# GNN layer pair: nodes laid across partitions by n % 128, bias by one-row products

## The chip, the core and the metric

The kernel runs on one core of a Trainium2 chip. The metric is the device time of one execution in microseconds, median of the runs. TensorE is called PE, VectorE DVE, ScalarE ACT, GpSimd POOL; SP is the engine that issues most DMAs.

## The reference

6250 nodes with 128 features, 200,000 edges sorted by destination, two residual layers in float32:

```
h = relu(layernorm(x))
ef  = (relu(edge_attr @ We1 + be1) @ We2 + be2) * sigmoid(ew * Wt + bt)
msg = relu(concat(h[src], ef) @ Wn1 + bn1) @ Wn2 + bn2
x = x + segment_sum(msg, dst) + h                     # layer 0
h = relu(layernorm(x))
agg = segment_sum(h[src], dst)
x = x + relu(relu((h + agg) @ W1 + b1) @ W2 + b2)     # layer 1
```

The kernel sums the messages before the product with Wn2, which is linear: `segment_sum(msg) = segment_sum(relu(...)) @ Wn2 + count * bn2`, where count is the number of edges that end in a node. This count times bias is one of the two things the change is about.

## The kernel before

The node features sit in SBUF as `xs` [128 partitions, NT = 49 tiles, 128 features], worked on in NG = 7 groups of GT = 7 tiles. Node n lies in partition n // 49, tile n % 49: partition p holds 49 nodes that follow one another. The sums over edges lie the other way round, features in partitions and nodes along the free axis: `acc` [128, 2, ...], where `acc[:, 0, n]` is the sum of node n and `acc[0, 1, n]` its edge count. One tile of nodes is therefore a view of `acc` with a step of 49 elements (`acc_group`).

The program has these stages; within an engine everything stands in a fixed order, and engines wait for one another on semaphores.

1. **Prologue.** SP loads `x` in 7 transfers of 448 KB (L370), then weights and index tables, all on one DMA queue. DVE takes statistics (L998), and later the window parameters (L1006 and on, which need edge bounds that went to DRAM and back); ACT normalizes (L590), PE multiplies by the node half of Wn1, DVE adds (L1034, L1038, L1042), and SP stores the product as `table0` in 7 transfers (L431). POOL gathers rows of `table0` by `src` (L525) once all are stored; SP reads tile bounds back (L434) after that too, and DVE waits for these.
2. **Layer 0 loop**, 49 bodies of four edge pairs: products, messages, one-hot sums into `acc`. For layer 1 it also counts edges per (source, destination window) in matrices `counts_d`, with keys made by `edge_keys` from the source's partition and tile.
3. **Transition.** After the last sum, ACT copies each group of `acc` into a contiguous stage (L670), PE multiplies a tile (stationary operand) by `wn2` (L857), DVE adds the product to `xs` (L1273). The counts of all nodes go by one DMA from one partition into 128 (L448, `count_n`), and DVE adds count times bias with 49 instructions (`add_bias`, L1264). DVE takes statistics (L1278). SP then reloads `acc[:, 1]` with stored count matrices (L354, 2940 KB), and POOL moves the edge keys (L562); both had waited for the DMA of the counts.
4. **Second table.** ACT normalizes again (L679), three bf16 parts of each value are made by ACT (L686), POOL (L565) and DVE (L1289, L1294), PE transposes (L866), DVE copies the transposed tile into `acc` as the new start (L1292). SP stores the parts as `table1` in 7 transfers of 672 KB through two buffers (L463); ACT may write a buffer again when its store has landed.
5. **Layer 1 loop.** PE sums gathered rows (L881) and products with count matrices (L891) while POOL gathers from `table1`.
6. **Output.** PE multiplies `w1` (stationary) with four and three tiles of `acc` as the moving operand (L937, L938), ACT applies relu (L719), PE multiplies by `w2` (L946), DVE adds (L1390, L1392), SP stores `out` (L494) in 7 transfers.

Of the kernel before, what the change touches and what calls it, by code (L numbers as in the profile page):

```python
# [10 lines left out]
ALU = mybir.AluOpType  # L11
# [3 lines left out]
P = 128  # L15
D = 128
# [70 lines left out]
def gnn_program(nc, x, ea, ew, src, src_tiles, dst_tiles, dst_blocks, We1, be1, We2, be2, Wt, bt, Wn1, bn1, Wn2, bn2,  # L87
                W1, b1, W2, b2, out):
    ctx = ExitStack()
    with ctx:  # L90
        def sb(name, shape, dt=F32):
            return ctx.enter_context(nc.sbuf_tensor(name, shape, dt))
# [25 lines left out]
        rstd = sb("rstd", [P, NT])  # L118
        count_n = sb("count_n", [P, NT])
        shift = sb("shift", [P, NT])  # L120
# [170 lines left out]

        acc_staged = sem("acc_staged")
        counts_moved = sem("counts_moved")
        x1_chain = sem("x1_chain")
        acc_zeroed = sem("acc_zeroed")
# [64 lines left out]
        def acc_group(g, which=0):  # L360

            v = acc[:, which, 0:N_PAD].rearrange("f (p t) -> f t p", t=NT)
            return v[:, bass.ds(g * GT, GT), :]


        @block.sync
        def _(sp):
            sp.dma_start(dst_b, dst_blocks).then_inc(dst_loaded, 16)
            for g in range(NG):
                sp.dma_start(xs[:, g * GT:(g + 1) * GT, :],  # L370
                             x[:, g * GT * D:(g + 1) * GT * D].rearrange("p (t d) -> p t d", d=D))\
                  .then_inc(x_loaded[g], 16)
                if g == 0:
                    sp.dma_start(dst_t[:, :], dst_tiles).then_inc(dst_tiles_loaded, 16)
# [52 lines left out]

            t0 = table0.rearrange("(p t) d -> p t d", t=NT)
            with sp.Fori(0, NG) as g:
# [17 lines left out]

            sp.dma_start(count_n[:, :], acc[0:1, 1, 0:N_PAD].rearrange("a (p t) -> a p t", t=NT)).then_inc(counts_moved, 16)  # L448

            sp.wait_ge(counts_moved, 16)  # L450
            for i in (0, 1):
# [7 lines left out]

            t1 = table1.rearrange("(p t) d -> p t d", t=NT)  # L460
            for g in range(NG):
# [28 lines left out]

            ov = out.rearrange("p (t d) -> p t d", d=D)
            with sp.Fori(0, NG) as g:
                sp.wait_ge(out_made, g + 1)
                sp.dma_start(ov[:, bass.ds(g * GT, GT), :], xs[:, bass.ds(g * GT, GT), :]).then_inc(out_stored, 16)  # L494
            sp.wait_ge(out_stored, 16 * NG)
# [3 lines left out]
        def _(pool):  # L499
# [58 lines left out]
            with pool.If(sweeps > 1):  # L558
                with pool.Fori(NBODY, sweeps * NBODY) as b:
                    gather_body(b)  # L560
            pool.wait_ge(counts_moved, 16)
            pool.tensor_copy(keys1, keys0).then_inc(keys_moved, 1)  # L562
# [14 lines left out]
        def _(act):  # L577
# [83 lines left out]
            with act.If(sweeps > 1):  # L661
                with act.Fori(1, sweeps) as s:
                    sweep(s, False)


            act.wait_ge(acc_added, sweeps * NB)
            for g in range(NG):
                if g >= 2:
                    act.wait_ge(upd_mm, g - 1)
                act.activation(stages[g % 2], acc_group(g), ACT.Copy).then_inc(acc_staged, 1)  # L670

# [51 lines left out]
        def _(pe):  # L723
# [126 lines left out]


            for g in range(NG):
                pe.wait_ge(acc_staged, g + 1)
                if g >= 2:
                    pe.wait_ge(x1_made, g - 1)
                for u in range(GT):
                    i = pe.matmul(p_prod[g % 2][:, u, :], stages[g % 2][:, u, :], wn2[:, :], start=True, stop=True)  # L857
                i.then_inc(upd_mm, 1)
# [92 lines left out]
        def _(dve):  # L951
# [206 lines left out]
            def edge_keys():  # L1158

                dve.wait_ge(src_loaded, 16)  # L1160
                src_b, key = src_b0[:, 0:NTILE], key0[:, 0:NTILE]
                chain(dve.tensor_scalar(src_b, src_i, 1.0 / NT, 0.5 / NT - 0.5, ALU.mult, ALU.add))
                settle()
                chain(dve.tensor_scalar(src_b, src_b, ROUND, None, ALU.add))
                settle()
                chain(dve.tensor_scalar(src_b, src_b, ROUND, None, ALU.subtract))
                settle()
                chain(dve.scalar_tensor_tensor(out=src_t, in0=src_b, scalar=-float(NT), in1=src_i,
                                               op0=ALU.mult, op1=ALU.add))
# [89 lines left out]

            dve.wait_ge(counts_moved, 16)  # L1260

            def add_bias(g):
                for t in range(g * GT, (g + 1) * GT):
                    i = dve.scalar_tensor_tensor(out=xs[:, t, :], in0=bn2_r[:, :], scalar=count_n[:, t:t + 1],  # L1264
                                                 in1=xs[:, t, :], op0=ALU.mult, op1=ALU.add)
                i.then_inc(x1_chain, 1)

            add_bias(0)
            for g in range(NG):
                x_g = xs[:, g * GT:(g + 1) * GT, :]  # L1270
                dve.wait_ge(upd_mm, g + 1)
                dve.wait_ge(x1_chain, g + 1)
                dve.tensor_tensor(x_g, x_g, p_prod[g % 2], ALU.add).then_inc(x1_made, 1)  # L1273
                if g < NG - 1:
                    add_bias(g + 1)
                dve.wait_ge(x1_made, g + 1)
                for t in range(g * GT, (g + 1) * GT):
                    i = dve.bn_stats(stats[:, t, :], xs[:, t, :])  # L1278
                i.then_inc(x1_stats, 1)
# [150 lines left out]
```

## Time and profile before

| | us |
|---|---|
| median of 3 runs (lowest, highest) | 3589.09 (3583.87, 3596.16) |
| profiled execution: time, span | 3590.76, 3589.0 |
| mean granted TensorE clock | 0.799 |
| busy: PE 2681.7 (75%), POOL 2068.4 (58%), DVE 1962.9 (55%), ACT 1004.6 (28%) | |
| transition, last sum to last statistics | 2593.9 to 2629.1 |
| second table, to the first product of layer 1 | to 2665.7 |
| output, first product to the end of the span | 3549.5 to 3589.0 |

The span runs from the first to the last instruction. Positions are microseconds from its start. The granted clock is the share of TensorE's full 2.4 GHz: 1.00 is 2.4 GHz and 0.50 is 1.2 GHz. A float32 product of 128 columns is two MATMUL records, each with its own weight load.

### The profile page before, as it was taken

How to read it: one execution, taken by the hardware profiler on the slowest of the kernel's cores; microseconds unless marked ns; L12 is line 12 of the kernel's file. 1: busy time of each engine (PE TensorE's matmuls, PEld its weight loads, DVE VectorE, ACT ScalarE, POOL GpSimd, SP SyncE). 2: the span in 40 equal slices, each digit the busy share in tenths (PEclk: the TensorE clock that was granted, in tenths of full speed). 3: DMA queues.
4: the chain of work that ended last, by engine and by line, in shares of the span. 5: the costliest groups of instructions: out<-in, count | busy, mean ns of one | idle time of the engine just before them, and what ended most of it. 6: DMA issues, size and time to landing. Idle time of an engine off the chain costs nothing.

```text
span 3589.0 us, 51735 instructions
## 1 busy us (share of the span) xinstructions
PE 2681.7 (75%) x14584; PEld 1614.4 (45%) x14585; DVE 1962.9 (55%) x4112; ACT 1004.6 (28%) x1000; POOL 2068.4 (58%) x2104
## 2 busy tenths in 40 slices
PE   4688878788777877788777877877745767666777
PEld 2444444444444444444434443433432544544554
DVE  7655655566565666566656666665763333233333
ACT  3233333333333333333333332322231111011111
POOL 4666666666566656666666566655324556555552
PEclk8788888788887887888888888888865766767778
DMA  5444444444343444344343443433222434334332
GB/s 188 110 124 134 130 132 126 128 127 135 121 127 122 126 122 123 121 126 123 122 124 124 122 123 121 124 106 118 48 94 84 152 99 129 104 111 126 117 103 62
DMA packets 229412, 426.77 MB, mean 119 GB/s; under 512 B 82703, under 2 KB 141584, under 8 KB 229072
## 3 DMA queue, kind: packets, MB, share of 16 engines
q0 software_dynamic: 74752, 153.23, 16.3%
q1 hardware_dynamic: 103152, 177.42, 15.0%
q10 hardware_dynamic: 51266, 93.34, 7.4%
q8 instruction: 97, 1.59, 0.2%
q14 instruction: 145, 1.19, 0.1%
HBM read 364.35 MB, written 59.43 MB: 118 GB/s over the span
## 4 chain that ended last, share of the span: by engine, by line
PE 41%; issue 20%; DVE 17%; another core or an unknown queue 11%; DVEq 9%; DMA 1%; SPq 0%; ACT 0%; ACTq 0%
PE ps L891 9%; PE ps L803 9%; PE ps L762 8%; PE ps L771 5%; DVE nodes L1152 5%; PE ps L782 4%; PE ps L754 3%; DVEq L1086 2%; DVEq L1132 2%; DVE arena L1152 2%; DVE hot L1107 1%; PE ps L881 1%; DVE acc L1094 1%; DVEq L1149 1%
## 5 line engine op out<-in xcount | busy, mean ns | idle before, releaser
L525 POOL DMA_INDIRECT big<-table,idx x2080 | 2044.2, 983 | 1391.8 <-issue 588.2
L803 PE MATMUL ps<-nodes 128*128 128x500 bf16 x1280 | 461.1, 476 | 348.7 <-issue 200.0
L762 PE MATMUL ps<-arena,we 128*128 128x512 f32 x784 | 516.4, 791 | 18.5 <-issue 13.3
L611 ACT ACTIVATE big<-big 128x1024 f32<-128x1024 f32 x196 | 207.1, 1057 | 1072.0 <-DVE big L1101 932.0
L782 PE MATMUL ps<-hot,big 128*128 128x64 f32 x3136 | 391.3, 274 | 99.4 <-issue 67.2
L1152 DVE TENSOR_SCALAR nodes<-iota_k,win_off,nodes 128x500 bf16<-128x500 f16 x1280 | 453.0, 405 | 0.0
L782 PEld LDWEIGHTS ps<-hot,big 128*128 128x128 f32 x3136 | 378.0, 194 | 102.2 <-issue 100.1
L1149 DVE TENSOR_TENSOR nodes<-iota_b,nodes 128x384 bf16<-128x384 f16 (+1 forms) x492 | 244.8, 497 | 278.6 <-remote 156.9
L803 PEld LDWEIGHTS ps<-nodes 128*128 128x128 bf16 x1280 | 107.6, 106 | 589.1 <-issue 308.0
L1101 DVE TENSOR_TENSOR big<-ps,big 128x1024 f32<-128x1024 f32 x196 | 239.0, 1219 | 225.5 <-issue 217.6
L601 ACT ACTIVATE arena<-ps,cols 128x1024 f32<-128x1024 f32 x196 | 218.6, 1115 | 405.3 <-PE ps L754 222.3
L692 ACT ACTIVATE arena<-ps 128x490 f32<-128x490 f32 x96 | 100.0, 1042 | 766.3 <-PE ps L806 656.5
L1094 DVE TENSOR_TENSOR acc<-ps,acc 128x128 f32 x392 | 113.6, 290 | 292.6 <-remote 244.3
L803 PE MATMUL ps<-arena 128*128 128x500 bf16 x384 | 170.6, 554 | 136.5 <-DVE arena L1152 96.1
L891 PE MATMUL ps<-acc,nodes 128*128 128x120 f32 x1568 | 222.7, 299 | 63.5 <-issue 56.2
L634 ACT ACTIVATE arena<-ps 128x490 f32<-128x490 f32 x192 | 199.0, 1037 | 227.8 <-remote 214.8
L1149 DVE TENSOR_TENSOR arena<-iota_b,arena 128x256 bf16<-128x256 f16 x192 | 80.8, 421 | 329.3 <-PE ps L803 187.3
L754 PE MATMUL ps<-arena,we 64*128 64x512 f32 x784 | 231.6, 664 | 24.6 <-DMA win_row<-win_d 17.6
L762 PEld LDWEIGHTS ps<-arena,we 128*128 128x128 f32 x784 | 174.0, 246 | 165.1 <-issue 160.2
L891 PEld LDWEIGHTS ps<-acc,nodes 128*128 128x128 f32 x1568 | 209.8, 215 | 72.8 <-issue 72.3
L606 ACT ACTIVATE arena<-arena,cols 128x1024 f32<-128x1024 f32 x196 | 240.9, 1229 | 0.0
L771 PEld LDWEIGHTS ps<-wn1b,ef 128*128 128x128 f32 x1568 | 188.2, 196 | 80.8 <-issue 80.8
(139 smaller groups left out, 2512.4 us busy)
## 6 DMA issues: line engine op xcount, KB each, us to landing
arena<-in_ew SPq DMA_DIRECT2D x196, 512.0 KB
arena<-in_ea SPq DMA_DIRECT2D x196, 256.0 KB
counts_d<-arena ACTq DMA_DIRECT2D x192, 245.0 KB
acc<-counts_d ACTq DMA_DIRECT2D x15, 2940.0 KB
big<-table,idx POOLq DMA_INDIRECT x2080
table<-big SPq DMA_DIRECT2D x7, 672.0 KB, 3.0
idx<-in_src SPq DMA_DIRECT2D x260, 4.0 KB
xs<-in_x SPq DMA_DIRECT2D x7, 448.0 KB, 8.7
```

What stands on the lines that cost most here:

```text
L525: pool.indirect_dma_start(to(u, q, t), None, table, bass.IndirectOffsetOnAxis(ap=idx[:, u, at:at + 1], axis=0))\
L601: act.activation(hid[:, :, :].rearrange("p q c -> p (q c)"), p_hid2, ACT.Relu, bias=be1_c).then_inc(hid_made, 2)
L606: act.activation(v, v, ACT.Sigmoid, bias=bt_c, scale=wt_c).then_inc(tw_made, 2)
L754: pe.matmul(p_hid[q], we1[k, :], ea_s[k, u, :], start=True, stop=True).then_inc(hid_mm, 1)
L762: pe.matmul(p_ef[q], we2[:, :], hid[:, q, :], start=True, stop=True).then_inc(ef_mm, 1)
L771: i = pe.matmul(p_pre[q][:, t * D:(t + 1) * D], efs[m][:, q, t * P:(t + 1) * P], wn1b[:, :], start=True, stop=True)
L782: pe.matmul(p_agg[:, q, 0, :], msg[:, m, q, t, :], hot_f[:, m, q, t, :], start=(t == 0), stop=(t == TB - 1))
L803: m = pe.matmul(to, hots[:, t, :], keys[:, t, :], start=False, stop=True, skip_group_check=True)
L891: m = pe.matmul(to, nodes[:, a, :], sums[:, :, a, :], start=(a == 0), stop=(a == NT - 1))
L1101: dve.tensor_tensor(msg[:, u % 2, :, :, :].rearrange("p q t d -> p (q t d)"), p_pre2, rows[:, u, :, :, :].rearrange("p q t d -> p (q t d)" ...
L1149: dve.tensor_tensor(hots[:, h * half:h * half + n, :], iota_v.to_broadcast([P, n, P]), half_src.to_broadcast([P, n, P]), ALU.is_equal)
L1152: m = dve.tensor_scalar(keys[:, h * half + t, :], iota_k[:, :], win_off[:, bass.ds(win, 1)], key[:, h * n + t:NTILE + VP][:, bass.ds(at, 1 ...
```

## The change

Node n now lies in partition n % 128 of tile n // 128. A tile of nodes is then 128 neighbours in `acc`, and the view of a group is contiguous. PE reads the sums straight from `acc` as stationary operand, with no copy by ACT. Edge count times bias is added on PE too: to each tile's product, a product with one contraction row (`edges[0:1]`, the counts, times one row of `bn2_r`) accumulates into the same PSUM tile; the DMA of the counts and `add_bias` on DVE are gone. A partition's share of a transfer of `x`, `table0`, `table1` and `out` is no longer one run of 7 nodes but 7 runs of one node: 512 bytes each, 768 in `table1`. DRAM rows stay in node order, so gathers read the same addresses. SP's reload of `acc[:, 1]` waits for all products with the counts; POOL's copy of the keys waits for PE to have passed the last sum (`keys_free`). `edge_keys` has the same instructions with its two results exchanged.

```diff
         def acc_group(g, which=0):
-            v = acc[:, which, 0:N_PAD].rearrange("f (p t) -> f t p", t=NT)
+            v = acc[:, which, 0:N_PAD].rearrange("f (t p) -> f t p", p=P)
             return v[:, bass.ds(g * GT, GT), :]
@@ block.sync
+            x_tiles, out_tiles = (a.rearrange("p c -> (p c)").rearrange("(t p d) -> p t d", p=P, d=D) for a in (x, out))
                 sp.dma_start(xs[:, g * GT:(g + 1) * GT, :],
-                             x[:, g * GT * D:(g + 1) * GT * D].rearrange("p (t d) -> p t d", d=D))\
+                             x_tiles[:, g * GT:(g + 1) * GT, :])\
-            t0 = table0.rearrange("(p t) d -> p t d", t=NT)
+            t0 = table0.rearrange("(t p) d -> p t d", p=P)
-            sp.dma_start(count_n[:, :], acc[0:1, 1, 0:N_PAD].rearrange("a (p t) -> a p t", t=NT)).then_inc(counts_moved, 16)
-            sp.wait_ge(counts_moved, 16)
+            sp.wait_ge(upd_mm, NG)
             for i in (0, 1):
                 sp.wait_ge(c_stored[i], 16 + 16 * (NW0 // 2))
             load_sums(sp, 0)
-            t1 = table1.rearrange("(p t) d -> p t d", t=NT)
+            t1 = table1.rearrange("(t p) d -> p t d", p=P)
-            ov = out.rearrange("p (t d) -> p t d", d=D)
-                sp.dma_start(ov[:, bass.ds(g * GT, GT), :], xs[:, bass.ds(g * GT, GT), :]).then_inc(out_stored, 16)
+                sp.dma_start(out_tiles[:, bass.ds(g * GT, GT), :], xs[:, bass.ds(g * GT, GT), :]).then_inc(out_stored, 16)
@@ block.gpsimd
-            pool.wait_ge(counts_moved, 16)
+            pool.wait_ge(keys_free, 1)
             pool.tensor_copy(keys1, keys0).then_inc(keys_moved, 1)
@@ block.scalar
-            act.wait_ge(acc_added, sweeps * NB)
-            for g in range(NG):
-                if g >= 2:
-                    act.wait_ge(upd_mm, g - 1)
-                act.activation(stages[g % 2], acc_group(g), ACT.Copy).then_inc(acc_staged, 1)
@@ block.tensor
+            pe.wait_ge(acc_added, sweeps * NB)
+            pe.sem_inc(keys_free, 1)
             for g in range(NG):
-                pe.wait_ge(acc_staged, g + 1)
                 if g >= 2:
                     pe.wait_ge(x1_made, g - 1)
+                sums, edges = acc_group(g), acc_group(g, 1)
                 for u in range(GT):
-                    i = pe.matmul(p_prod[g % 2][:, u, :], stages[g % 2][:, u, :], wn2[:, :], start=True, stop=True)
+                    pe.matmul(p_prod[g % 2][:, u, :], sums[:, u, :], wn2[:, :], start=True, stop=False)
+                    i = pe.matmul(p_prod[g % 2][:, u, :], edges[0:1, u, :], bn2_r[0:1, :], start=False, stop=True)
                 i.then_inc(upd_mm, 1)
@@ block.vector
-            dve.wait_ge(counts_moved, 16)
-            def add_bias(g):
-                for t in range(g * GT, (g + 1) * GT):
-                    i = dve.scalar_tensor_tensor(out=xs[:, t, :], in0=bn2_r[:, :], scalar=count_n[:, t:t + 1],
-                                                 in1=xs[:, t, :], op0=ALU.mult, op1=ALU.add)
-                i.then_inc(x1_chain, 1)
-            add_bias(0)
             for g in range(NG):
                 x_g = xs[:, g * GT:(g + 1) * GT, :]
                 dve.wait_ge(upd_mm, g + 1)
-                dve.wait_ge(x1_chain, g + 1)
                 dve.tensor_tensor(x_g, x_g, p_prod[g % 2], ALU.add).then_inc(x1_made, 1)
-                if g < NG - 1:
-                    add_bias(g + 1)
                 dve.wait_ge(x1_made, g + 1)
                 for t in range(g * GT, (g + 1) * GT):
                     i = dve.bn_stats(stats[:, t, :], xs[:, t, :])
```

On DVE in the transition, before: `xs<-bn_r,count_n,xs` is `add_bias`, seven tiles at a time, `xs<-xs,ps` the addition of a group's product, `BN_STATS` the statistics.

```order
L1264 SCALAR_TENSOR_TENSOR xs<-bn_r,count_n,xs 128x128 x7
L1273 TENSOR_TENSOR xs<-xs,ps 128x896
L1264 SCALAR_TENSOR_TENSOR xs<-bn_r,count_n,xs 128x128 x7
L1278 BN_STATS stats<-xs 128x6 x7
L1273 TENSOR_TENSOR xs<-xs,ps 128x896
```

Now only the addition and the statistics of each group are left on DVE. On PE in the same place, the new order is, for each of 49 tiles, a product with `wn` and one with the bias row `bn_r`, both with `acc` as the other operand (before, these were 49 products `ps<-wn,big` in a row, from the stage):

```order
L840 REGISTER_ALU
L847 MATMUL ps<-wn,acc 128x128
L848 MATMUL ps<-bn_r,acc 128x128
L847 MATMUL ps<-wn,acc 128x128
L848 MATMUL ps<-bn_r,acc 128x128
```

The number of products doubles, from 49 to 98. On SP behind the layer 0 loop, before, the DMA of the counts stands ahead of the reload of `acc`, the index loads and the seven stores of `table1`:

```order
L448 DMA count_n<-acc 128x1x49
L354 DMA acc<-counts_d 128x12x490
L457 ISA
L457 DMA idx<-in_src 128x8
L463 DMA table<-big 128x2688 x7
```

And now, where the stores name 7 runs of 384 elements a partition instead of one of 2688:

```order
L444 REGISTER_ALU
L351 DMA acc<-counts_d 128x12x490
L453 ISA
L453 DMA idx<-in_src 128x8
L459 DMA table<-big 128x7x384 x7
```

The reload keeps its place in the queue, but the wait ahead of it is now for the last product of the transition.

## Rows read from the trace of the kernel before

**Rows 1.** Timeline of the prologue: start, length, engine, line, operation [idle before].

```profile
11.17 9.56 DVE L998 BATCH_NORM_STATS2 stats<-xs 128x6 f32<-128x128 f32 x49
27.25 0.56 DVE L1006 TENSOR_TENSOR big<-great_all,base_all 1x392 int32<-1x392 int32 x1 [3.86 <-DMA base_all<-base_d]
57.42 2.82 POOL L525 DMA_INDIRECT big<-table,idx  x1 [41.79 <-DMA table<-nodes]
```

**Rows 2.** Stretches of the prologue: last columns clock, DMA share, GB/s.

```profile
10.00:15.00 5.00, 0.00 (x0) 0.00 (x0) 4.97 (x23) 0.00 (x0) 5.00 (x1) 1.00 1.02 404
15.00:15.50 0.50, 0.00 (x0) 0.00 (x0) 0.50 (x4) 0.00 (x0) 0.50 (x1) 1.00 1.02 329
16.00:16.50 0.50, 0.00 (x0) 0.00 (x0) 0.50 (x4) 0.00 (x0) 0.00 (x0) 1.00 1.23 285
```

**Rows 3.** Timeline of the transition.

```profile
2593.89 3.47 ACT L670 ACTIVATE big<-acc 128x896 f32<-128x896 f32 x2 [4.31 <-DVE acc L1094]
2595.82 5.75 PE L857 MATMUL ps<-wn,big 128*128 128x128 f32 x28 [2.83 <-ACT big L670]
2596.75 0.40 SPq L354 DMA_DIRECT2D acc<-counts_d  x1
2596.78 2.81 POOL L562 COPY arena<-nodes 128x3148 f32<-128x3148 f32 x1 [15.20 <-DMA count_n<-acc]
2596.88 4.44 DVE L1264 SCALAR_TENSOR_TENSOR xs<-bn_r,count_n,xs 128x128 f32<-128x128 f32 x7 [3.02 <-DMA count_n<-acc]
...
2606.61 1.92 DVE L1264 SCALAR_TENSOR_TENSOR xs<-bn_r,count_n,xs 128x128 f32<-128x128 f32 x7
2608.44 1.44 DVE L1278 BATCH_NORM_STATS2 stats<-xs 128x6 f32<-128x128 f32 x7
2609.80 1.07 DVE L1273 TENSOR_TENSOR xs<-xs,ps 128x896 f32<-128x896 f32 x1
...
2627.66 1.45 DVE L1278 BATCH_NORM_STATS2 stats<-xs 128x6 f32<-128x128 f32 x7
```

**Rows 4.** Stretches of the transition, columns as in rows 2.

```profile
2595.00:2600.00 5.00, 4.18 (x19) 4.21 (x20) 3.12 (x3) 3.17 (x3) 2.81 (x1) 0.50 0.49 122
2600.00:2605.00 5.00, 3.37 (x24) 3.01 (x23) 4.90 (x17) 3.29 (x3) 0.00 (x0) 0.92 1.04 395
```

**Rows 5.** Groups over the whole span: busy us, mean ns; two weight loads, and two copies of the same size.

```profile
L803 PEld LDWEIGHTS ps<-nodes 128*128 128x128 bf16 x1280 | 107.6, 106 | 589.1 <-issue 308.0 <-DVE nodes L1152 240.2
L797 PEld LDWEIGHTS ps<-zeros 1*128 1x128 bf16 x288 | 26.9, 94 | 53.8 <-issue 29.7
L1292 DVE COPY acc<-ps 128x896 f32<-128x896 f32 x7 | 12.2, 1738 | 0.0
L1038 DVE COPY ef<-ps 128x896 f32<-128x896 f32 x4 | 4.3, 1082 | 0.0
```

**Rows 6.** The chain through two groups of the second table: start, length, what.

```profile
2639.37 3.00 DMA table<-big
...
2643.43 1.09 DVE big L1289
...
2647.12 3.00 DMA table<-big
```

**Rows 7.** The chain through one group of the output, and one product of the loop.

```profile
2559.85 1.91 PE ps L762 x4
...
3557.81 1.82 PE ps L937 x2
3559.63 1.37 PE ps L938 x2
...
3575.24 1.56 PE ps L946 x14
```

**Rows 8.** A stretch at the start of the output, columns as in rows 2.

```profile
3553.00:3554.00 1.00, 1.00 (x3) 0.40 (x2) 0.00 (x0) 0.90 (x1) 0.00 (x0) 0.93 0.00 0
```

**Rows 9.** PE between 2676.6 and 2711.6 us, by groups.

```profile
L891 PE MATMUL ps<-acc,nodes 128*128 128x120 f32 x18 | 5.4, 360 | 12.7 <-issue 12.3
```

More of the change, by code:

```diff
@@ L118, in gnn_program @@
         rstd = sb("rstd", [P, NT])
-        count_n = sb("count_n", [P, NT])
         shift = sb("shift", [P, NT])
@@ L290, in gnn_program @@
         out_chain = sem("out_chain")
-        acc_staged = sem("acc_staged")
-        counts_moved = sem("counts_moved")
-        x1_chain = sem("x1_chain")
+        keys_free = sem("keys_free")
         acc_zeroed = sem("acc_zeroed")
@@ L1161, in edge_keys @@
                 src_b, key = src_b0[:, 0:NTILE], key0[:, 0:NTILE]
-                chain(dve.tensor_scalar(src_b, src_i, 1.0 / NT, 0.5 / NT - 0.5, ALU.mult, ALU.add))
+                chain(dve.tensor_scalar(src_t, src_i, 1.0 / P, 0.5 / P - 0.5, ALU.mult, ALU.add))
                 settle()
-                chain(dve.tensor_scalar(src_b, src_b, ROUND, None, ALU.add))
+                chain(dve.tensor_scalar(src_t, src_t, ROUND, None, ALU.add))
                 settle()
-                chain(dve.tensor_scalar(src_b, src_b, ROUND, None, ALU.subtract))
+                chain(dve.tensor_scalar(src_t, src_t, ROUND, None, ALU.subtract))
                 settle()
-                chain(dve.scalar_tensor_tensor(out=src_t, in0=src_b, scalar=-float(NT), in1=src_i,
+                chain(dve.scalar_tensor_tensor(out=src_b, in0=src_t, scalar=-float(P), in1=src_i,
                                                op0=ALU.mult, op1=ALU.add))
```

## The prediction

> **What bounds the kernel now.** I read the timeline first, to find the places that the change touches, then for each the chain that ended last and the stretches with the granted clock and the DMA rate. Both edge loops are left as they are: gathers read the same DRAM rows, and `edge_keys` and the one-hot work have the same instructions and shapes. So the time can change in four places only: prologue, transition, second table and output, together some 160 us of the 3589.
>
> In the **transition** the last sum is in `acc` at 2593.9. PE starts on the first stage at 2595.8; DVE gets the counts at 2596.9, and its first seven bias additions take 4.44 us beside POOL's copy of the keys, against 1.92 for seven later on [rows 3]. From then on DVE has no gap: bias 1.92, statistics 1.44, addition 1.07, about 4.2 us a group with the overlaps of their ends. The last statistics end at 2627.66 + 1.45 = 2629.1. DVE is the bound there; PE and ACT wait for it.
>
> In the **second table** the chain goes round through two buffers: store 3.00, ACT, DVE L1289, DVE L1292, DVE L1294, next store, 7.75 us for two groups [rows 6]. The copy L1292 takes 1.74 us, while L1038 copies the same 896 columns out of PSUM in 1.08; the difference is the step of 49 elements in the destination [rows 5].
>
> In the **output** PE is on the chain without a gap: L937 1.82, L938 1.37, L946 1.56, so 4.75 us a group [rows 7]. L937's two instructions read 512 columns each with that same step, 0.91 us apiece, while L762 puts four instructions of 512 contiguous float32 columns into 1.91 us, with the last one's tail: about 0.43 apiece when the clock is full.
>
> **The change part by part.** Everything is summed against the profiled execution (3590.76 us, span 3589.0); the median of the three runs is 1.7 us lower.
>
> *A, loads of x.* Runs of 512 bytes instead of 3584. In the queue, big runs go at 404 GB/s from 10 to 15 us; at 15 us the weights begin, which are rows of 512 bytes, and the rate falls to 329, later to 285 as tiny columns mix in, with the engines fully busy [rows 2]. I take 320: 7 x 448 KB = 3.21 MB take 10.0 us instead of 8.0. DVE's statistics of x run without a gap from 11.2 to 20.7 and cover their own loads, even 2 us later. But everything queued behind x on SP's queue comes later too: weights, index tables, and the edge bounds, which go to DRAM and back, and on whose return DVE's L1006 waits at 27.25 [rows 1]. DVE does nothing else before that, so +2.0 us. Bounds: 0 and, at 285 GB/s, +3.3.
>
> *B, stores of table0.* They have the time of the pipeline to go out; only the last one is on the path (POOL's first gather waits for it [rows 1]): 459 KB at 320 instead of 404 GB/s, +0.3.
>
> *C, transition.* Gone: ACT's copies, the DMA of the counts, the 49 additions. Added: 98 MATMUL records for 49 one-row products. No row shows a float32 product with one contraction row. The nearest say that rows don't shorten it: a weight load of 1 x 128 takes 94 ns, one of 128 x 128 takes 106 [rows 5]. I take the full product's price; the lower bound is nothing, the upper is that a change between 1 and 128 rows stops the overlap of load and product, some 0.3 us a record. PE can begin at 2593.95. The clock has fallen to half there; before, it came back 5 us after PE began: 28 records took 5.75 us [rows 3, 4]. So 24 of the 196 records at 0.205 us until 2599, and 172 at the full clock's pace of the output, 1.56 / 14 = 0.111: 19.2 us, PE's end at 2618.2. A group is 3.1 us on PE and 2.5 on DVE (1.07 + 1.44), so DVE keeps up and adds its last group behind PE: 0.2 + 1.07 + 1.45 gives 2620.9 to 2621.2. Against 2629.1 that is **-7.9 us**. PE, not DVE, is then the bound. POOL's copy of the keys comes right at the start, where DVE is idle. The reload of `acc[:, 1]` on SP's queue moves from 2596.8 to 2618.3. Before, its 2940 KB were in at about 2606.7, ten microseconds after issue [rows 3, 4]; now they are in near 2628.5, and the first table store behind it on the queue is due at 2631.5, so this stays hidden with 3 us to spare. What waits behind it besides are four small index loads, due much later.
>
> *D, second table.* L1292 writes contiguously: -0.66 us, of which 0.43 reach L1294, since POOL's part of the group ends then. The store has 768-byte runs: from 512 bytes at 320 GB/s (25.6 ns a run on one of 16 engines) and 5376 at 404 (213 ns) a line gives 35 ns, 56 of them 1.9 us instead of 1.7, so the 3.00 become 3.27. First turn -0.43, three more at -0.43 + 0.27: **-0.9**. Bounds: -1.5 with no loss in the stores, +2 if a store lands 1 us later.
>
> *E, output.* L937 to 0.86, L938 to 0.65 us a group: -1.67. The group is then 3.08 us on PE; DVE's two additions (each the size of L1273's 1.07) stay under that. But PE comes to the output with half the clock, which rises at 3553.1, 3.5 us after the first product at 3549.5 [rows 8]. At half the clock contiguous columns would take 0.86 us an instruction, twice the 0.43, hardly less than the 0.91 of the strided ones. So the first group wins 0.2 and the second loses a little: 6 x 1.67 + 0.2 - 0.3 = **-9.9**. Bounds: -11.7 with the full clock at once, -8 if it takes twice as long.
>
> *F, last store of out.* On the path, as B: +0.3.
>
> Sum: 2.0 + 0.3 - 7.9 - 0.9 - 9.9 + 0.3 = -16.1. 3590.8 - 16.1 = 3574.7, and 1.7 less for the median: about 3574.
>
> The size of the runs is where the Trainium skill speaks otherwise: "DMA: Bandwidth & Descriptors", section Specifications, gives 512 bytes as the least transfer for line rate. By that A, B and F would be nothing and the time 3571. The row has 329 GB/s against 404, and I go by the row.
>
> **The rivals.**
>
> *The clock stays low in the transition.* PE now runs without a break, which speaks for the full clock; but before, with its breaks, it was granted 0.50 and then 0.92 in two stretches there [rows 4]. All 196 records at 0.21 us are 41 us: PE's end 2635, the statistics' 2638, C is +9 instead of -7.9, and the time 3591: no change. 6 in 100.
>
> *A pause of PE, the slower side.* PE has stretches in which it issues hardly anything and waits for nothing that the profile names. The longest stands right behind the place of the change: between 2676.6 and 2711.6 it gets through 18 products of L891 in 35 us, with 12.3 us idle put down to "issue" ahead of them [rows 9]. If such a pause falls into the transition's doubled run of products, where PE is now alone on the path, it costs its full length; from 27 us on the kernel is slower by over 0.3%, and one of 35 us gives 3609. Against it: POOL is gathering back to back in that stretch, and idle in the transition. 6 in 100.
>
> *That pause shrinks*, since PE's stream is 98 products longer ahead of it and comes to it otherwise. PE's chain goes through it, so up to 30 us more would be won: 3545 to 3565. 12 in 100.
>
> *The step is not what slows the output.* Then E is nothing, and D only the stores: 3584, no change by the measure below. For it: no row shows these two lines with another layout. Against: ACT's copy with the step takes 1.74 us and more (3.47 for two [rows 3]), DVE's 1.74, both well above their contiguous likes. 10 in 100.
>
> *Forecast*, 3574 with its own range 3567 to 3582: 62 in 100. What is left, 4, is short DMA runs that are much slower than the weights' (half rate: A +8, D +5), about 3588.
>
> **How the numbers follow.** A change of this kernel can be told from none by about 0.3%, 11 us, so faster means under 3578. The forecast's own spread leaves it there 9 times in 10: 56, and the shrunken pause 12 make 0.69. Same: the rest of the forecast 6, low clock 5, step 9, short runs 4: 0.24. Slower: 0.07. The range leaves out half of the shrunken pause and the slower side: 3559 to 3590.
>
> **What would show it.** L937's duration per instruction near 0.6 us instead of 1.1 and seven groups 3.1 us apart; L1292 at 1.08; PE's last bias product near 2618 on the scale of before, at a clock of 1.00 from 5 us after its start; the reload landed before the first store of `table1` is issued; L1006 two microseconds later. Wrong it would be if the one-row products cost more than full ones, if the stores of short runs land a microsecond or more later, or if PE's pauses fall otherwise.

## The result, and the profile after

The changed kernel takes 3636.07 us (median of five, 3627.78 to 3646.90) against 3589.09 us (3583.87 to 3597.29): a ratio of 1.0132, 95% interval 1.0103 to 1.0161. It is 47 us slower where 15 us faster was forecast, and outside the range. The profiled execution is the fastest of the five: 3627.78 us, span 3626.0 us, so the two profiles differ by 37.0 us only. The table divides these 37.0; each row is a difference between marks of the two timelines.

| stretch | forecast | measured |
|---|---|---|
| prologue, to L1006, now L997 (A) | +2.0 | +6.4 |
| from there to the first gather (B) | +0.3 | +0.5 |
| layer 0 loop | 0 | +3.8 |
| transition, last sum to last statistics (C) | -7.9 | **+38.4** |
| second table, to the first row sum (D) | -0.9 | -1.0 |
| layer 1 loop | 0 | -1.7 |
| output, with the last store (E, F) | -9.6 | -9.4 |

**Prologue.** Timeline of the changed kernel (start, length, engine, line, operation, idle before), where [rows 1] stand for the kernel before:

```profile
2.34 10.89 SPq L368 DMA_DIRECT2D xs<-in_x  x6
10.55 9.60 DVE L989 BATCH_NORM_STATS2 stats<-xs 128x6 f32<-128x128 f32 x49
13.27 1.45 SPq L374 DMA_DIRECT2D wn1a<-in_Wn  x1
23.05 0.42 SPq L386 DMA_DIRECT2D base_d<-least  x1
33.61 0.55 DVE L997 TENSOR_TENSOR big<-great_all,base_all 1x392 int32<-1x392 int32 x1 [10.82 <-DMA base_all<-base_d]
```

and a stretch of it (the last columns are the clock, the DMA share and GB/s):

```profile
6.00:14.00 8.00, 0.00 (x0) 0.00 (x0) 7.97 (x22) 0.00 (x0) 8.00 (x1) 1.00 1.14 319
```

The rate is the forecast's 320 GB/s. The statistics are not delayed. But SyncE needs 10.89 us to issue six loads of x, and only then come the weights and, at 23.05 us, the first store of block bounds. The same two rows in the kernel before:

```profile
2.17 4.47 SPq L370 DMA_DIRECT2D xs<-in_x  x6
16.43 0.42 SPq L388 DMA_DIRECT2D base_d<-least  x1
```

VectorE waits 10.8 us for the bounds, where it waited 3.9 [rows 1].

**Transition.** The same timeline at its start, and further on the addition that stands for L1273 of [rows 3]:

```profile
2603.91 0.72 DVE L1085 TENSOR_TENSOR acc<-ps,acc 128x128 f32 x2 [2.87 <-PE ps L773]
2604.77 0.77 PE L847 MATMUL ps<-wn,acc 128*128 128x128 f32 x2 [1.01 <-DVE acc L1085]
2605.47 0.50 PEld L848 LDWEIGHTS ps<-bn_r,acc 1*128 1x128 f32 x2 [0.23 <-issue]
2605.47 0.79 PE L848 MATMUL ps<-bn_r,acc 1*128 1x128 f32 x2
2606.19 0.50 PEld L847 LDWEIGHTS ps<-wn,acc 128*128 128x128 f32 x2 [0.23 <-issue]
2606.19 0.80 PE L847 MATMUL ps<-wn,acc 128*128 128x128 f32 x2
...
2675.74 1.09 DVE L1254 TENSOR_TENSOR xs<-xs,ps 128x896 f32<-128x896 f32 x1 [7.55 <-PE ps L848]
2675.78 0.38 SPq L351 DMA_DIRECT2D acc<-counts_d  x1
```

Each product has two records. A product starts every 0.72 us, from the first to the last, whichever its kind; PEld is idle 0.23 us ahead of each. From the start of the first product to that of the last record it is 70.5 us. VectorE waits 7.55 us for the last group. And the clock stayed at its lower level (1.2 GHz), as the stretches show, where [rows 4] has 0.92 within ten microseconds:

```profile
2600.00:2605.00 5.00, 3.98 (x18) 3.73 (x19) 1.61 (x3) 0.51 (x1) 0.21 (x1) 0.50 0.01 3
2605.00:2675.00 70.00, 70.00 (x195) 48.23 (x195) 15.23 (x48) 0.00 (x0) 2.59 (x1) 0.50 0.00 1
```

PE counts as busy for the whole 70 us: the busy share alone does not show that each product takes more than three times its time.

**Second table and output.** One store in the chain that ended last (start, length, what), for [rows 6]:

```profile
2695.70 3.25 DMA table<-big
```

and timeline rows for L1292 of [rows 5] and for the output's groups of [rows 7]:

```profile
2689.49 1.08 DVE L1271 COPY acc<-ps 128x896 f32<-128x896 f32 x1
...
3602.54 1.02 PE L928 MATMUL ps<-acc,w 128*128 128x512 f32 x2
...
3605.61 1.02 PE L928 MATMUL ps<-acc,w 128*128 128x512 f32 x2
```

The copy takes 1.08 us, the store 3.25, and an output group 3.07: these three steps went as forecast.

### The profile page after: what moved, and what is told of

It reads as the page before. It is cut to its first block, busy times and chain, and to the rows that moved or that the text cites. A ratio compares the mean times of both kernels' runs of the same rounds, so it can differ in the third digit from the quotient of the medians.

```text
span 3626.0 us, 51863 instructions
## 1 busy us (share of the span) xinstructions
PE 2731.1 (75%) x14682; PEld 1643.1 (45%) x14683; DVE 1945.5 (54%) x4063; ACT 992.3 (27%) x993; POOL 2066.5 (57%) x2104
## 4 chain that ended last, share of the span: by engine, by line
PE 40%; issue 20%; DVE 17%; another core or an unknown queue 11%; DVEq 10%; DMA 1%; SPq 1%; ACT 0%; POOL 0%; ACTq 0%
PE ps L882 9%; PE ps L791 8%; PE ps L750 7%; PE ps L759 5%; DVE nodes L1143 5%; PE ps L770 4%; DVEq L1077 3%; PE ps L742 3%; DVEq L1123 2%; DVE hot L1098 2%; DVE arena L1143 2%; DVE acc L1085 2%; DVEq L1140 1%; PE ps L872 1%
## 5 line engine op out<-in xcount | busy, mean ns | idle before, releaser
L770 PE MATMUL ps<-hot,big 128*128 128x64 f32 x3136 | 383.6, 274 | 80.1 <-issue 44.4
L759 PEld LDWEIGHTS ps<-wn1b,arena 128*128 128x128 f32 x1568 | 186.3, 194 | 90.9 <-issue 88.2
```

The costliest lines, as they stand in the source:

```text
L759: i = pe.matmul(p_pre[q][:, t * D:(t + 1) * D], efs[m][:, q, t * P:(t + 1) * P], wn1b[:, :], start=True, stop=True)
L770: pe.matmul(p_agg[:, q, 0, :], msg[:, m, q, t, :], hot_f[:, m, q, t, :], start=(t == 0), stop=(t == TB - 1))
```

## The experiments

Times are from four chips. The kernel before takes 2891 to 2896 us on three of them and 3659 us on the fourth, so only ratios to it, measured on the same chip, are given. The first four versions share a chip; so do 64 rows, the unaltered kernel, loads on ScalarE's queue and old runs; so do one part alone, the same with full rows, the strided operand and the split; and so do the last three. Lengths of a stretch are from the profiles, one execution each; a time for the 98 products goes from the first start to the last. Line numbers are those of the changed kernel, a few lines off in some variants.

Theory 1 was formed from the timeline above: a weight load with another number of rows than the product ahead of it waits for it, and costs a piece of time at each change. Its rivals: two products that add into one PSUM tile (2), the stationary operand read from `acc` unstaged (3), a price of every one-row product (5).

**Full rows.** The bias product takes all 128 rows; rows 1 to 127 of the counts are zero.

```diff
-  i = pe.matmul(p_prod..., edges[0:1, u, :], bn2_r[0:1, :], start=False, stop=True)
+  i = pe.matmul(p_prod..., edges[:, u, :], bn2_r[:, :], start=False, stop=True)
```

> One edit to the changed kernel: the bias product takes all 128 rows of the edge counts and of the bias (rows 1 to 127 of the counts are zero, so the sum is the same) where it took one row. Theory 1 (a change between 128 rows and one row stops the overlap of a weight load with the product before it, at every product, and the clock stays at 1.2 GHz with it): the 98 products of the transition fall from 0.72 us each (70.9 us in all) to 2 records of about 0.11 us at 2.4 GHz or 0.215 at 1.2 GHz, so 21 to 42 us, and the kernel from 3636 to 3586 to 3607 us. Theory 2 (it is that two products add into one tile of PSUM) and theory 3 (it is that the stationary operand is taken from the accumulator unstaged): no difference, 3636 us.

Measured: 2879.72 us, ratio 0.9964 (0.9949 to 0.9978). Two stretches of its transition:

```profile
2120.00:2125.00 5.00, 4.08 (x22) 4.11 (x23) 0.29 (x1) 0.00 (x0) 2.80 (x1) 0.56 0.03 7
2125.00:2145.00 20.00, 19.68 (x177) 19.49 (x175) 15.52 (x49) 0.00 (x0) 0.00 (x0) 1.00 0.01 2
```

The 98 products take 23.5 us instead of 70.5. The first 15 records run at the lower clock, from 2120.9 to 2124.1 us, then it is at its upper level (2.4 GHz). The last statistics start 27.0 us after the last sum (before: 35.3, the changed kernel: 73.7). Theories 2 and 3 fall: both features are still there. The kernel is faster than before.

**Grouped.** The same products, seven of sums and then seven of one row:

```diff
   for u in range(GT):
-      pe.matmul(p_prod..., sums[:, u, :], wn2[:, :], start=True, stop=False)
-      i = pe.matmul(p_prod..., edges[0:1, u, :], bn2_r[0:1, :], start=False, stop=True)
+      pe.matmul(p_prod..., sums[:, u, :], wn2[:, :], start=(u % 4 == 0), stop=False)
+  for u in range(GT):
+      i = pe.matmul(p_prod..., edges[0:1, u, :], bn2_r[0:1, :], start=False, stop=(u in (3, GT - 1)))
```

> The changed kernel with the same products in another order: in each group the seven products of sums first, then the seven one-row products, so 14 changes of the number of rows in the whole transition instead of 98. Theory 1 (price per change of rows): 14 changes at 0.3 to 0.5 us remain of 98, so nearly as fast as with full rows, 3590 to 3612 us. Theory 5 (price per one-row product, whatever stands beside it): no difference, 3636 us. Theory 2 (two products into one tile, back to back): as theory 1; full rows against this one tells them apart.

Measured: 2880.98 us, ratio 0.9957 (0.9944 to 0.9970); 34.9 us for the 98 products. Timeline of PE, groups of 14 records at either clock:

```profile
2120.54 3.35 PE L849 MATMUL ps<-bn_r,acc 1*128 1x128 f32 x14
2123.82 3.36 PE L847 MATMUL ps<-wn,acc 128*128 128x128 f32 x14
...
2143.56 1.82 PE L849 MATMUL ps<-bn_r,acc 1*128 1x128 f32 x14
2145.32 1.83 PE L847 MATMUL ps<-wn,acc 128*128 128x128 f32 x14
```

```profile
2117.00:2139.00 22.00, 21.72 (x93) 20.41 (x94) 6.98 (x22) 0.00 (x0) 2.80 (x1) 0.50 0.01 2
2141.00:2152.00 11.00, 11.00 (x90) 10.28 (x90) 7.62 (x24) 0.00 (x0) 0.00 (x0) 1.00 0.01 2
```

Groups of one row and of 128 rows take the same 3.28 us, then 1.76. So a one-row product has no price of its own (theory 5 falls); what is paid is the change. The stage is 11.3 us longer than with full rows (38.3 against 27.0 to the last statistics), yet the two medians are 1.3 us apart: the profiled execution, 2888.33 us, is one of the slowest of ten. Whether the clock rises sooner in the others no trace shows, so the argument rests on the stage and not on the ratio.

**One row only.** Both products have one row; the sums are left out.

> The changed kernel with the product of sums replaced by a second one-row product of bias and edge count: it leaves out the sums (their part of the layer is missing from the output), and all 98 products have one row. Theory 1 (change of rows): no change of rows is left, 98 products at 0.22 to 0.43 us, 3586 to 3607 us. Theory 5 (each one-row product pays): all 98 pay, 3636 us or more. Theory 2 (two products into one tile): 3636 us.

Measured: 2895.84 us, ratio 1.0021 (1.0010 to 1.0032); 41.7 us. Timeline and a stretch:

```profile
2125.92 0.63 PE L847 MATMUL ps<-bn_r,acc 1*128 1x128 f32 x2
2126.34 0.63 PE L848 MATMUL ps<-bn_r,acc 1*128 1x128 f32 x2
```

```profile
2115.00:2155.00 40.00, 40.00 (x190) 40.00 (x189) 15.23 (x48) 0.00 (x0) 1.66 (x1) 0.50 0.00 1
```

Without changes a product starts every 0.42 us, but the clock stays at its lower level for all 40 us, PE busy throughout. So there are two prices. At the lower clock a change costs 0.72 - 0.42 = 0.30 us, and a group of 14 in the grouped version says the same: 3.28 - 14 x 0.213 = 0.30. At the upper clock it costs 1.76 - 14 x 0.112 = 0.19. (A record takes 40.0 / 190 = 0.21 here, and 20.0 / 177 = 0.113 with full rows.) And the clock: 196 records at 0.213 instead of 0.112 are 20 us. Together 97 x 0.30 + 20 = 49 us, less 15 x 0.10 = 1.5 for the records that run at the lower clock with full rows too: 47.4, against 47.0 measured between the changed kernel and full rows.

**No bias.** The one-row products are left out, and with them count times bias.

> The changed kernel without the 49 one-row products: it leaves out the bias times the edge count. Theory 1: the 49 products of sums, taken from the accumulator unstaged, take 2 records of 0.11 to 0.215 us each, 10 to 21 us in all in place of 70.9, and the kernel takes 3576 to 3587 us. Theory 3 (the unstaged operand is what is slow): 49 x 0.72 = 35 us, 3600 us.

Measured: 2869.30 us, ratio 0.9927 (0.9910 to 0.9943). The 49 products take 16.0 us, paced by VectorE. So the unstaged sums are not what is slow; theory 3 falls again.

**64 rows.** `edges[0:64, u, :]` and `bn2_r[0:64, :]` in the changed kernel.

> The changed kernel with 64 rows in the bias product instead of one (rows 1 to 63 of the counts are zero, so the sum is the same). Theory 1 as it stands now (a weight load with another number of rows than the product before it waits for that product to end: 0.35 us a record at 1.2 GHz instead of 0.213): 64 rows against 128 pay the same, 98 products in 70 us at 1.2 GHz, or, if the clock rises, less. Theory 6 (what counts is how many rows are idle, for the clock alone): the products pay for each change, but the granted clock rises above 0.50 during the stretch.

Measured: 2923.90 us in one run. Groups of instructions (busy us, mean ns):

```profile
L848 PE MATMUL ps<-bn_r,acc 64*128 64x128 f32 x98 | 38.9, 498 | 0.0
L847 PE MATMUL ps<-wn,acc 128*128 128x128 f32 x98 | 38.8, 500 | 1.4 <-DVE acc L1085 1.4
```

Again 70.5 us at a clock of 0.50. The pace does not go by the single row: it is that the two numbers differ. Theory 6, that with fewer rows idle the clock would rise, falls for 64 rows. Whether the changes hold the clock down here or the idle rows do, as with one row only, is not shown: no run has a stream of 64 rows alone.

**The changed kernel on a faster chip**, unaltered.

> The changed kernel itself, unaltered, timed against the kernel before on one chip with the next three, since the kernel before took 2892 us on the chip of the four runs above and 3589 us in the first comparison, and only ratios to the kernel before can be set side by side. If the cause lies in the transition's 98 products (70.5 us against 23.5 us with full rows), it stands 47 us above the version with full rows (0.9964 of the kernel before), at a ratio of 1.0126 where the kernel before takes 2892 us, with pitches of a record of 0.35 us and a granted clock of 0.50. If that price belonged to the first chip alone, the ratio is near 0.996 here.

Measured: 2926.56 us, ratio 1.0101 (1.0077 to 1.0125), 7 us under the 1.0126 expected; 70.5 us for the products, as on the first chip. The gap of 7 us is not explained; the stage is the one that was expected.

**One part alone, in the kernel before.** One-row products in place of `add_bias`; order, staging, strides and the DMA of the counts as before. The reload of `acc` waits for the products, as in the changed kernel.

```diff
-  i = pe.matmul(p_prod..., stages[g % 2][:, u, :], wn2[:, :], start=True, stop=True)
+  pe.matmul(p_prod..., stages[g % 2][:, u, :], wn2[:, :], start=True, stop=False)
+  i = pe.matmul(p_prod..., edges[0:1, u, :], bn2_r[0:1, :], start=False, stop=True)
```

> The kernel before with one part of the change alone: the one-row product of edge counts and bias on TensorE in place of VectorE's 49 multiply-adds, with the old node order, the staging by ScalarE and strided counts kept. Theory 1 (changes of the number of rows): 98 products at 0.72 us = 70.5 us from the first product, where the kernel before has its last statistics 33 us after it, so some 37 us slower: a ratio of 1.012 to 1.014. If the loss needs the unstaged sums or the new order: a ratio of 0.996 to 1.001.

Measured: 2930.91 us, ratio 1.0132 (1.0113 to 1.0151); 71.0 us for the products. The transition's loss comes whole with this one part: 39.8 us, where some 37 were expected.

**The same with full rows.**

> As the one-row version of the kernel before, with all 128 rows in the product. Theory 1: 98 products in 23.5 us or, paced by ScalarE's staging, about 30 us, so not slower than the kernel before and up to 8 us faster: a ratio of 0.997 to 1.000. If strided weights cost as strided moving operands do, up to 15 us more: 1.002.

Measured: 2894.78 us, ratio 1.0012 (1.0000 to 1.0023): the expectation's main figure missed, its second branch, slow strided weights, met. Groups of PE's weight loads:

```profile
L860 PEld LDWEIGHTS ps<-bn_r,acc 128*128 128x128 f32 x98 | 25.4, 307 | 0.0
L859 PEld LDWEIGHTS ps<-wn,big 128*128 128x128 f32 x98 | 16.8, 212 | 3.1 <-issue 3.1
```

In the old order the counts are a stationary operand with a step of 49 elements; a load of them takes 307 ns against 212 from the contiguous stage, and the 98 products 33.3 us instead of 23.5. It is not ScalarE's staging that holds PE up: PE waits for it only once, 2.8 us ahead of the first group. So the bias product pays only together with the new order of nodes.

**A strided moving operand in the output.** Full rows, and the output's first products read `acc` with the old step (sums of other nodes, so the output is not the reference's).

> Full rows in the bias product, and the first product of the output stage takes its moving operand in steps of 49 columns, as the kernel before does (so it takes the sums of other nodes, and the output is not the reference's). The term E of the prediction (a moving operand of step 49 takes twice as long as one whose columns lie side by side): a 512-column record goes from about 0.43 back to 0.91 us in pitch, the stage is 10 us longer than with full rows alone, and the ratio goes from 0.9964 to about 1.000. If E came from the stores of the output instead: no difference, 0.9964.

Measured: 2890.66 us in one run, 0.9999 of the kernel before on its chip where about 1.000 was expected, and 10.9 us above full rows on another chip of about the same speed. The groups of its profile, and under it of full rows:

```profile
L928 PE MATMUL ps<-acc,w 128*128 128x512 f32 x14 | 14.1, 1094 | 0.9 <-DVE acc L1288 0.9
```

```profile
L928 PE MATMUL ps<-acc,w 128*128 128x512 f32 x14 | 8.2, 671 | 0.9 <-DVE acc L1288 0.9
```

From the first of these products to the last group's it is 28.0 us instead of 18.9, with the new runs of `out` in both. Term E is the step of the moving operand.

**Loads of x on ScalarE's queue.** With full rows:

```diff
-  sp.dma_start(xs[:, g * GT:(g + 1) * GT, :], x_tiles[...]).then_inc(x_loaded[g], 16)
+  act.dma_start(xs[:, g * GT:(g + 1) * GT, :], x_tiles[...]).then_inc(x_loaded[g], 16)
```

> Full rows in the bias product, and the seven loads of x issued from ScalarE's queue instead of SyncE's, with the same tiles and the same 512-byte runs. Theory A1 (the prologue's 6.8 us are time that SyncE's queue takes to issue loads of 896 runs each, ahead of the weights and of the stores of block bounds): the stores of bounds go out at 16 to 18 us instead of 23 us, the first gather starts at 57.5 us or a little earlier instead of 64.3 us, and the kernel is 6 to 7 us faster than full rows alone (2880 us with the kernel before at 2892 us): 2873 us, a ratio of 0.994. Theory A2 (it is the data rate of 512-byte runs that delays what is behind them on the 16 DMA engines): the first gather stays at 63 to 64.3 us and the ratio at 0.9964.

Measured: 2872.15 us, ratio 0.9923 (0.9900 to 0.9946). Timeline:

```profile
0.75 17.84 ACTq L575 DMA_DIRECT2D xs<-in_x  x7
11.51 1.45 SPq L381 DMA_DIRECT2D base_d<-least  x1
60.90 2.73 POOL L515 DMA_INDIRECT big<-table,idx  x1 [45.28 <-DMA table<-nodes]
```

The bounds go out at once, but the seven loads now need 17.8 us to issue and x itself is late: the first gather moves from 65.5 to 60.9, not to the 57.5 expected. Theory A2 had it at 63 to 64.3, and falls here.

**Old runs.** With full rows, x loaded as the kernel before does (its nodes in other partitions than the rest takes them to be; output not the reference's).

> Full rows in the bias product, and x loaded from SyncE's queue as the kernel before does, one run of 3584 bytes per partition (so the nodes of x lie in other partitions than the rest of the kernel takes them to be, and the output is not the reference's; times are not touched by it). Both theories of the prologue: the first gather is back at 57.5 us, and the ratio is 0.994. If the gather stays at 64.3 us, neither of them holds.

Measured: 2869.33 us, ratio 0.9914 (0.9890 to 0.9939), first gather at 59.1 us, not 57.5. But the two versions above that load x as before (one part alone, on a chip as fast as this one) have it at 58.4 and 59.2 us, so 59.1 is the whole way back. The short runs are the loss.

**Split over two queues.** Loads 0, 2, 4, 6 from SyncE's, the others from ScalarE's.

> Full rows in the bias product, and the loads of x split over two queues: groups 0, 2, 4 and 6 from SyncE's, 1, 3 and 5 from ScalarE's. With all seven on ScalarE's queue their issue took 17.8 us there (0.75 to 18.6), the statistics waited for the later tiles, and the first gather started at 60.9 us against 65.5 us with all on SyncE's and 59.1 us with the old runs of 3584 bytes. Theory A1 (issue time of a queue): four loads on SyncE's take some 7 us, three on ScalarE's some 5 to 8, the first gather starts at 57.5 to 60 us, and the ratio to the kernel before is 0.991 to 0.993. Theory A2 (the 16 DMA engines set the pace of short runs whichever queue issues them): not before 60.9 us.

Measured: 2875.92 us, ratio 0.9942 (0.9924 to 0.9959), first gather at 65.0 us. Theory A1 falls: SyncE has three loads fewer to issue and is hardly earlier. Its first store of bounds goes out at 23.0 us, against 23.5. The line of theory A2, not before 60.9, is met here, but it fell in the version before last and falls in the next. So the issue time is not work of SyncE's. What fits is that a queue which holds many short runs lets no further transfer in until the DMA engines have worked some off; that is a reading of these issue times, and no run shows the queue's state.

**Bounds on ScalarE's queue.** With full rows; x and weights stay on SyncE's.

```diff
-  sp.wait_ge(base_made, 2)         # with 4 stores, the wait for them, 2 loads back
+  act.wait_ge(base_made, 2)        # the same seven lines, on ScalarE
```

> Full rows in the bias product, all seven loads of x and the weights on SyncE's queue as in the changed kernel, and the four stores of block bounds and the two loads that bring them back on ScalarE's queue, which has nothing to do there. Theory A3 (the short runs keep SyncE's queue and the DMA engines busy to about 19 us, but VectorE's 11.8 us of waiting comes from the bounds alone, which stand behind x and the weights in SyncE's queue): the stores go out at 11.3 us, as soon as they are made, instead of 23.5 us, the bounds are back at about 23 us, and the first gather starts at 55 to 58 us instead of 65.5 us (biases and weights, which land at 27 us, are late next): a ratio of 0.992 to 0.9935, where full rows alone stand at 0.9964. Theory A2 (the data rate alone): small stores queue behind the x runs on the 16 DMA engines, the bounds are not back before 28 us, and the first gather is at 60 us or later.

Measured: 3627.86 us with the kernel before at 3658.93, ratio 0.9910 (0.9883 to 0.9936). Timeline:

```profile
10.82 0.62 ACTq L568 DMA_DIRECT2D base_d<-least  x1
13.43 1.46 SPq L374 DMA_DIRECT2D wn1a<-in_Wn  x1
18.57 0.46 ACTq L578 DMA_DIRECT2D base_all<-base_d  x1
23.23 0.55 DVE L998 TENSOR_TENSOR big<-great_all,base_all 1x392 int32<-1x392 int32 x1
55.51 2.73 POOL L509 DMA_INDIRECT big<-table,idx  x1 [39.89 <-DMA table<-nodes]
```

Theory A3 holds: x and weights are as late as in the changed kernel, the bounds are back before VectorE asks for them (no wait stands at L998), and the first gather starts at 55.5 us: 10.1 us earlier than full rows on the same chip (below), and 1.9 earlier than [rows 1], which are from another chip. This version beats both kernels. Its median is 20 us under that of full rows there; the prologue explains 10 of them, the layer 0 loop is 5.3 us shorter in this profile, which is within its scatter, and the rest is not accounted for.

**Full rows once more**, on this fourth chip.

> The version with full rows in the bias product once more, beside the next two on one chip: 0.9964 of the kernel before, as the first time, and the transition's 98 products in 23.5 us.

Measured: 3648.12 us, ratio 0.9968 (0.9953 to 0.9983); 24.6 us for the products, 28.1 from the last sum to the last statistics, first gather at 65.6 us.

**Short runs alone, in the kernel before** (x in other partitions than it takes them to be; output not the reference's).

> The kernel before with one part of the change alone: x is loaded in 512-byte runs (nodes to other partitions than this kernel takes them to be, so the output is not the reference's). If the short runs are the whole of the loss in the prologue, whatever stands elsewhere: the first gather 6 to 7 us later than in the kernel before, at 64 to 65 us, and a ratio of 1.0023. If it took the new node order elsewhere too: less.

Measured: 3669.11 us, ratio 1.0030 (1.0009 to 1.0051), first gather at 64.5 us, 7.0 later than [rows 1]; A and B together measured +6.9. The short runs of x alone bring all of it.

## Why the prediction was wrong

**The step that failed is in C:** "The nearest say that rows don't shorten it ... I take the full product's price". The price of a single one-row product is right: fourteen of them take as long as fourteen of 128 rows. Wrong is that the price was taken per product and not per pair of neighbours. The rows it was read from [rows 5] are mean lengths of a weight load, and a load that waits for the product ahead of it is no longer for that. The upper bound named the mechanism, "some 0.3 us a record", without a sum. Read as the pace of all 196 records it is 59 us, against 70.5 measured; read as added to each, it is 59 us more, and measured are 0.30 us for each change, one a product, 29 us in all. It was kept as a bound and got no chance among the rivals, and the range did not reach it.

A sign of the wait stood in the kernel before. Its loop has a one-row product (L806) behind four of 128 rows, and one of 128 rows (L762) behind that. Timeline:

```profile
2576.07 0.13 PEld L803 LDWEIGHTS ps<-nodes 128*128 128x128 bf16 x2
2576.08 1.85 PE L803 MATMUL ps<-nodes 128*128 128x500 bf16 x4
2576.47 0.15 PEld L803 LDWEIGHTS ps<-nodes 128*128 128x128 bf16 x1 [0.27 <-issue]
2576.89 0.15 PEld L803 LDWEIGHTS ps<-nodes 128*128 128x128 bf16 x1 [0.26 <-issue]
2577.85 0.10 PEld L806 LDWEIGHTS ps<-zeros 1*128 1x128 bf16 x1 [0.82 <-issue]
2577.86 0.18 PE L806 MATMUL ps<-zeros 1*128 1x2 bf16 x1
2577.97 0.50 PEld L762 LDWEIGHTS ps<-arena,we 128*128 128x128 f32 x2
2577.97 3.15 PE L762 MATMUL ps<-arena,we 128*128 128x512 f32 x4
```

The four products start at 2576.08, 2576.47, 2576.89 and 2577.30. The loads for the third and fourth start at 2576.47 and 2576.89, with the second and third product, so one product ahead of their own. The one-row load does not: it starts at 2577.85, with its own product, and so does the load of 128 rows behind it. A loop's end stands between L803 and L806, so the row count is not shown to be the cause at this place; but the place to look was a pair of neighbours, not a mean.

**The low clock was a rival, at 6 in 100,** priced as if alone: 41 us for the records. That is what it is with one row only (41.7). It came together with the price of the changes. The argument against it, "PE now runs without a break, which speaks for the full clock", held with 128 rows throughout, where the clock rose 3.2 us after the first product, and failed here: PE counted as busy for 70 us at half the clock, and got through a record in 0.36 us where 0.21 is the pace at that clock without changes. Why few rows or changes of them keep the clock down stays open.

With 128 rows in both products C is what was forecast: the last statistics start 27.0 us after the last sum against 35.3 in the kernel before, -8.3 for -7.9. On the fourth chip it is 28.1 against 35.8 (short runs alone, which has the transition of before), -7.7. The changed kernel with full rows is at 0.9964 and 0.9968, 11 to 13 us faster than before, where -15 was forecast; the 4.4 us that A takes beyond its forecast cover the difference.

**A was too small, +6.4 for +2.0, and outside its bounds.** The rate was right (319 GB/s). The step that failed is "everything queued behind x on SP's queue comes later too ... so +2.0 us", which carries the lateness of the data over to the queue behind it. SyncE issues the first load of x in 0.44 us, and the six behind it take 10.89 us (4.47 in the kernel before); the weights stand behind, and then the bounds. The runs show the place (bounds on another queue bring all of it back) and that it isn't SyncE's own time (split). That an issue lasts until the queue has room is argued from this, and how many runs a queue holds was not measured.

**Right:** B (+0.5 for +0.3), D (-1.0 for -0.9, with a store of 3.25 for 3.27), E and F (-9.4 for -9.6, with 3.07 us a group for 3.08), the reload of `acc[:, 1]` hidden before the first table store, and that a pause of PE would not fall into the transition. "That pause shrinks" did not come, and had 12 in 100: the pause is still there, moved by the 48 us that everything moved by. A stretch of it, where [rows 9] stand for before:

```profile
2726.00:2760.00 34.00, 6.39 (x22) 4.42 (x22) 0.00 (x0) 0.00 (x0) 21.91 (x24) 0.55 0.27 70
```

A slip that changes nothing: the forecast's sum, 3574.7 less 1.7, is 3573 and not 3574.

**Not explained:** the layer 0 loop is 3.8 us longer between the two profiles. Among twelve profiles on the three faster chips, whose kernels differ outside it, this loop takes 2047.9 to 2056.3 us from the first gather to the last sum. So a difference of this size is within the scatter between executions and chips.

The Trainium skill, "TensorE: Matmul & The Clock Gate", section "LDWEIGHTS (loading the stationary operand)", says that the time of a weight load goes by its columns, not by its rows. The grouped products agree in their pace, 3.28 us for either kind. The same page of the Trainium skill, section "Part 3: Packing small matmuls — row/col tiling", has a load overlap products in flight only where its row group differs. These runs show otherwise for whole streams: loads of equal row counts overlap the products, 0.11 us a record, and a change of the count costs 0.19 to 0.30 us.

## What to carry to other kernels

A product with few contraction rows costs no less than a full one, and next to products of 128 rows it costs more. Pad it to 128 with zeros, if they are there (23.5 us here), or gather the short ones, so that the count changes rarely (34.9 us); and look for its price in a pair of neighbours, not in a mean. Read a stream's pace from starts that follow one another and the clock's column, since the busy share was full at a third of the speed (70.5 us against 23.5). When a load gets shorter runs, look at what stands behind it on its queue, and put a short round trip that someone waits for on a queue that is idle.

## What was not expected of the hardware

- A change between 128 rows and 64 or one cost 0.30 us at the lower clock; at the upper one, measured for a single row alone, 0.19. Streams with such changes at each product, and streams of one-row products alone, stayed at 0.50 for 40 to 70 us; with changes every 14 records the clock rose only after about 22 us, and with 128 rows throughout after 3.2.
- Strided weights cost more, as strided moving operands do: 307 ns against 212 for a 128 x 128 load with a step of 49 float32 elements.
- A load of x with 896 runs of 512 bytes takes 1.8 us of SyncE's issue, from the second on (10.89 us for six; 4.47 with runs of 3584 bytes), and 2.5 us on ScalarE's beside a busy SyncE (17.84 for seven).
- The kernel before takes 2891 to 2896 us on three chips and 3589 and 3659 us in the other comparisons. On one of the faster ones, with full rows, the pause of PE behind the transition is gone: in 11 us PE works through 109 records, where the stretch of 34 us above holds 22.

```profile
2186.00:2197.00 11.00, 10.13 (x109) 10.00 (x107) 0.53 (x3) 0.00 (x0) 8.26 (x10) 1.00 0.34 79
```
